# One attention layer with 16 small heads: biases after each half of the scores, row-maximum work at new places, the second half of each load behind the row maxima

## The reference

```python
q, k, v = (layernorm(x) @ W.T + b)                    # 16 heads of 8 columns each
sim  = q k^T + scale * rel_emb[bucket(i - j)]         # causal, 1024 x 1024 for each head
attn = softmax(sim)                                   # row maxima vary: the weights are large
x    = x + (attn @ v) @ Wo.T + bo
h    = relu(layernorm(x) @ w1[0] + b1[0])             # only expert 0 has weight
x    = x + layernorm_gamma_beta(layernorm(x) + h @ w2[0] + b2[0])
```

## Time and profile before

| what | value |
|---|---|
| median of 3 runs | 407.93 us (404.85, 410.7, 407.93) |
| the profiled execution | 402.29 us, of which span 400.5 us |
| PE busy | 321.0 us (80%) |
| DVE busy | 287.5 us (72%) |
| ACT busy | 184.0 us (46%) |
| mean granted TensorE clock | 0.92 of full |

### The profile page before, as it was taken

How to read it: one execution, slowest core, us unless ns; L and a number is a source line. 1 busy time by engine, 2 the same in 40 slices (tenths; PEclk the granted TensorE clock), 3 DMA queues, 4 the chain that set the end, 5 groups by cost and what they waited for, 6 DMA issues and landing times.

```text
span 400.5 us, 8158 instructions
## 1 busy us (share of the span) xinstructions
PE 321.0 (80%) x3197; PEld 153.1 (38%) x3197; DVE 287.5 (72%) x960; ACT 184.0 (46%) x258; POOL 69.5 (17%) x78
## 2 busy tenths in 40 slices
PE   0182438396999899799889979988988998999982
PEld 0131215143334335334434433443443344337752
DVE  3985356358668589588678848967875996773986
ACT  1042024131655554575565545556555545873330
POOL 9812035700001000100100100010010000161552
PEclk9996586668699999999999989999998999999998
DMA  8013422410012101201201220331222010100011
GB/s 227 26 53 116 145 90 95 148 64 3 2 43 66 39 18 52 81 1 61 75 12 44 68 64 2 86 88 26 65 79 55 15 16 12 33 2 10 5 52 53
DMA packets 18295, 21.97 MB, mean 55 GB/s; under 512 B 5584, under 2 KB 14960, under 8 KB 18256
## 3 DMA queue, kind: packets, MB, share of 16 engines
q1 hardware_dynamic: 18256, 21.45, 18.5%
HBM read 14.98 MB, written 4.23 MB: 48 GB/s over the span
## 4 chain that ended last, share of the span: by engine, by line
PE 51%; DVE 17%; DMA 15%; ACT 7%; issue 5%; SPq 4%; POOL 1%; DVEq 0%; POOLq 0%; ACTq 0%
PE ps L1015 14%; PE ps L1044 13%; PE ps L1001 13%; DMA QA<-mrow 7%; ACT PT L626 6%; PE ps L1032 5%; DMA qk_scratch<-QS 4%; DVE FM L759 3%; DVE XN L701 2%; DVE junk L766 2%; DMA KA<-qk_scratch 2%; DMA rows<-in_vectors 2%; PE ps L1077 2%; DVE st L836 1%; DVE U L889 1%
## 5 line engine op out<-in xcount | busy, mean ns | idle before, releaser
L626 ACT ACTIVATE PT<-ps 128x1024 f32<-128x1024 f32 (+1 forms) x192 | 145.8, 810 | 132.4 <-PE ps L1032 101.9
L759 DVE TENSOR_REDUCE FM<-ps 128x1 f32<-128x512 f32 (+3 forms) x176 | 108.4, 660 | 29.2 <-PE ps L1001 29.1
L1001 PE MATMUL ps<-KA,QA 96*128 96x256 bf16 (+3 forms) x544 | 108.7, 294 | 17.6 <-DMA KA<-qk_scratch 14.3
L1015 PE MATMUL ps<-QA,KA 98*128 98x512 bf16 (+3 forms) x384 | 99.0, 343 | 25.4 <-DMA QA<-mrow 10.3
L766 DVE CUSTOM_DVE_ANT_0 junk<-ps,NB 128x256 bf16<-128x256 f32 (+1 forms) x224 | 78.8, 403 | 37.3 <-PE ps L1001 37.2
L1044 PE MATMUL ps<-PT,VG 128*16 128x512 f32 (+3 forms) x768 | 86.9, 498 | 0.0
L1001 PEld LDWEIGHTS ps<-KA,QA 96*128 96x128 bf16 x544 | 44.1, 101 | 103.7 <-DVE FM L759 32.9
L1015 PEld LDWEIGHTS ps<-QA,KA 98*128 98x128 bf16 x384 | 32.5, 101 | 52.5 <-ACT PT L626 21.6
L497 POOL COPY NB<-NBH 128x1024 bf16<-128x1024 bf16 x7 | 7.3, 1040 | 212.3 <-PE ps L1044 211.4
L1032 PE MATMUL ps<-TT,flb 128*32 128x176 f16 (+4 forms) x1152 | 38.9, 245 | 0.0
L1032 PEld LDWEIGHTS ps<-TT,flb 128*32 128x32 bf16 x1152 | 21.5, 96 | 17.9 <-issue 17.0
(11 more groups left out here) (88 smaller groups left out, 255.5 us busy)
## 6 DMA issues: line engine op xcount, KB each, us to landing
QA<-qk_scratch SPq DMA_DIRECT2D x48, 96.0 KB
KA<-qk_scratch SPq DMA_DIRECT2D x16, 288.0 KB
TT<-f_scratch SPq DMA_DIRECT2D x16, 120.0 KB, 7.8
qk_scratch<-QS SPq DMA_DIRECT2D x4, 384.0 KB
qk_scratch<-QS SPq DMA_DIRECT2D x12, 128.0 KB
X<-in_x SPq DMA_DIRECT2D x2, 512.0 KB, 6.2
out<-U SPq DMA_DIRECT2D x4, 256.0 KB, 2.3
xnT<-OT SPq DMA_DIRECT2D x28, 32.0 KB
```

The lines of the kernel that those rows point to most:

```text
L626: nc.scalar.activation(PT[:, s % 3, 2 * q:2 * q + 2, off:off + w], ST[:, q, :, off:off + w], ACT.Exp).then_inc(s_exp, 1)
L759: nc.vector.tensor_reduce(FM[:, ib, heads[0]:heads[-1] + 1, piece], bank[:, 0:w * len(heads)].rearrange("p (h n) -> p h n", n=w), AX.X, AL ...
L1001: last = nc.tensor.matmul(bank[:, i * w + j - j0:i * w + j - j0 + n], QA[0:KS, p, ib // 4, h, (ib % 4) * 128:(ib % 4 + 1) * 128], KA[0:KS, ...
L1015: last = nc.tensor.matmul(ST[:, q, h % 2, off:off + w], KA[0:KST, p, jb // 4, h, (jb % 4) * 128:(jb % 4 + 1) * 128], QA[0:KST, p, ic, h, o ...
```

## The change

1. `biases` takes the half q and is called right after `scores(.., q)`. Before, the biases of both halves came after both score halves.
2. The positions of the units: pos 0 is now after half 0's scores and biases, pos 1 lies behind the values (right ahead of pos 2) and gets nothing from the new planner in the groups 1 to 7, whose cost list is changed with it. With the new constants unit 0 is at (0, 2), unit 10 at (4, 2), units 35 and 36 at (10, 2), unit 37 at (11, 0), and unit 38 alone at the next group's (0, 0). In group 0, whose units are placed by the same even spread as before, unit 37 of group 1 comes to (11, 2).
3. `move_m` is one transfer of two rows.
4. The second half of the load, with TT, of group g + 1 is issued in group g behind the move of group g's half 1. Before, it was issued at the end of group g - 1. Groups 0 and 1 are loaded in full at the start, as before.

```diff
-        half = 2 * step_cols(ic, jb)[1] + (640 if near_cols(ic, jb) else 0)
-        for pos, cost in enumerate((half, half, 4.2 * step_cols(*STEPS[s])[1])):
+        half = 2 * step_cols(ic, jb)[1] + (850 if near_cols(ic, jb) else 0)
+        rest = 4.2 * step_cols(*STEPS[s])[1] + 240
+        for pos, cost in enumerate((half + rest / 2, 0, half + rest / 2)):
...
-S_START, S_END, M1_AT = 0.15, 1.03, 1.06
+S_START, S_END, M1_AT = 0.09, 0.965, 1.0
...
             def move_m(p, half, g):
-                for part in range(2):
-                    sp.dma_start(QA[MROW + part:MROW + part + 1, p, half, :, :],
-                                 mrow[4 * part:4 * part + 4, half, :]).then_inc(s_md[half], 16)
+                sp.dma_start(QA[MROW:MROW + 2, p, half, :, :], mrow[:, half, :]).then_inc(s_md[half], 16)
...
                 move_m(p, 1, g)
+                if g:
+                    second_half(g + 1, (g + 1) % GPB, 1 - p)
                 for k in sums[:1]:
                     gather_all(k)
                 move_m(1 - p, 0, g + 1)
...
-                wait_apart(sp, s_str, 2 * NSTEP * g + 2 * NSTEP)
-                load_half(g + 2, p, 1)
+
+            def second_half(g, hg, p):
+
+                sp.wait_ge(s_str, 2 * NSTEP * (g - 1))
+                load_half(g, p, 1)
                 load_tt(hg, p)
...
             move_m(0, 1, G - 2)
+            second_half(G - 1, GPB - 1, 1)
             gather_all(4)
...
                     if at:
                         scores(*at, 0)
+                        biases(*at[1:], 0)
                     s_units_at(s, 0)
                     if at:
                         scores(*at, 1)
-                    s_units_at(s, 1)
-                    if at:
-                        biases(*at[1:])
+                        biases(*at[1:], 1)
                     if s == 0:
                         pe.wait_ge(s_vg, g + 1)
                     values(g, p, s)
+                    s_units_at(s, 1)
                     s_units_at(s, 2)
```

More of the change, by code:

```diff
@@ L1011, in scores @@
                 if q == 0 and jb == 0:
-                    pe.wait_ge(s_md[ic], 32 * g + 32)
+                    pe.wait_ge(s_md[ic], 16 * g + 16)
                 pe.wait_ge(s_exp, 2 * NSTEP * g + 2 * s + q + 1)
@@ L1020, in scores, with biases @@
                     last.then_inc(s_str, 1)
-            def biases(p, s):
+            def biases(p, s, q):
                 ic, jb = STEPS[s]
@@ L1026, in biases @@
                 near = near_cols(ic, jb)
[L1027 to L1035, removed]
+                if not near:
+                    return
+                for h in range(2 * q, 2 * q + 2):
+                    for c, u0, n in near:
+                        for e in range(2):
+                            r0 = 64 * c + 32 * e
+                            last = nc.tensor.matmul(ST[r0:r0 + 32, q, h % 2, off:off + n], flb[:, 32 * e:32 * e + 32],
+                                                    TT[:, p, h, u0:u0 + n], start=False, stop=True,
+                                                    skip_group_check=True)
+                last.then_inc(s_str, 1)
             def values(g, p, s):
@@ L1155, in _ @@
                 scores(0, 0, 0, q)
+                biases(0, 0, q)
                 unit(0, 0, OWN0 + q)
-            biases(0, 0)
             group(0, 0, 1, first=True)
```

## The result

The changed kernel takes 414.11 us in the median of four runs (413.31 to 415.24); the kernel before, run beside it four times, takes 406.39 us. The ratio is 1.023, with a 95% interval of 1.013 to 1.033. Some executions of a kernel lie over 1.5% above its fastest, and all ratios here leave them out: 1.023 is 414.11 over the 404.85 us of the other three runs of before. The forecast was 405.6 us and no measurable change. The profiled execution took 413.31 us, of which 411.5 us are the span: 11.0 us more than the span of before.

What follows compares the result with a forecast made beforehand. PE was taken as busiest, with holes at seams and row moves. Ahead of the periods - 3.8, six periods + 0.6, behind them + 0.9: - 2.3 us from 407.93 gave 405.6 us; range 394 to 416 us.

Steps and rivals of the forecast that it cites:

- the head: Ahead of the start of group 1's half-1 row move: shorter waits, summing to - 3.8 us.
- the tail: Behind the start of group 7's half-1 row move: more work left, less some waits, + 0.9 us.
- Seam holes and the mrow wait gone: Each period: PE's holes at the seam of two groups (1.25 us) and for the row move (1.6 us) go.
- The load lands at T + 11.5 us, a wait of 2.3 us at unit 10: Groups 1 to 6: load lands 11.5 us after the half-1 row move starts (T); PE needs it at 9.2, waits 2.3.
- I take 0: Splitting biases by half: operand type changes on PE bounded at 0 to 0.1 us a step, taken as 0.
- I add 0.2 us: Ahead of the half-1 row move: PE waits 0.2 us for DVE's maxima, from bounds of 0 and 1 us.
- The period: From one group's half-1 row move start to the next: 32.4 us before the clock is counted, 33.8 us with it.
- The clock, 1.4 us in each of six periods: After the wait at unit 10 the granted clock falls to 0.50, adding 1.4 us to each period.
- Clock kept: Rival: the wait at unit 10 is no longer than 1.42 us, or is borne; 397.2 us, chance 0.17.
- clock stays down: Rival: each wait at unit 10 brings some 9 us at clock 0.50; 424 us, chance 0.15.
- Gathers, 0.8 us in groups 4 to 6: Eight gather transfers right behind the load add 0.8 us to each of these three periods, making 34.6 us.
- The early exponential gives nothing: Rival: at the seam PE waits for the exponential's second half or DVE's maxima instead; 414.0 us, chance 0.08.

Runs made afterwards that it cites:

- POOL's early copy: The changed kernel with POOL's copy of NB released by the end of the group's maxima, ahead of the copy of V: 408.3 us, ratio 1.009.

## Why the prediction was wrong, step by step

The forecast of the periods was + 0.6 us and they took + 9.0; the head was to give 3.8 us and gave 0.1; the tail was to cost 0.9 and cost 2.1. The measured ratio of 1.023 lies above the 2% that the prediction took for the least that can be told, with an interval that begins at 1.013; the time lies inside the range.

- **Seam holes and the mrow wait gone:** right. Both are missing from the timeline in every group from 1 on.
- **The load lands at T + 11.5 us, a wait of 2.3 us at unit 10:** right in mechanism and nearly in size. It lands 11.7 us behind T, and PE is ready about 0.5 us later than at my 9.2; two switches lie in between. The wait is 1.70 to 2.11 us as shown. (The tail of "some 80 GB/s" is that of the windows from 197 to 200, at 76 to 82 GB/s and shares of 0.19 and 0.20; the row quoted for it has 52 GB/s at 0.18.)
- **The split, "I take 0":** this step failed, and it is the largest term. The bounds of 0 to 0.1 us a step were read off a row in which the biases are followed by values. The cost arises when a score matmul or unit follows, and again at the way back into the biases, which the change makes happen nine times a period: 0.15 us each by its busy time, 1.35 us a period, 8.1 us for the six. The upper bound was no bound, because the row did not contain the transition in question.
- **"I add 0.2 us" for DVE at unit 38:** this failed by 0.9 us a period (0.89 us shown, 1.06 with the matmul's overlap), at the upper end of the bounds. The cause was not that the units follow each other more closely but POOL's copy of NB, which the group's last values release, and these now stand behind unit 37. I had followed PE, DVE and SP past the moved units, and not POOL's queue. The bound had been read as a slack of DVE, not as what else runs then.
- **The period:** forecast 32.4 us without the clock, measured 34.85. It shows best in the part behind unit 10, for group 2 of the changed kernel and group 3 of before:

```profile
177.29:200.54 23.25, 22.32 (x250) 8.90 (x254) 19.27 (x56) 12.97 (x16) 1.39 (x2) 1.00 0.08 28
```

```profile
208.49:231.10 22.61, 21.59 (x260) 9.48 (x259) 19.29 (x63) 12.54 (x17) 1.39 (x2) 1.00 0.16 53
```

  Forecast for it were 20.9 us, measured 23.25; T to unit 10 was forecast at 11.5 and took 11.6 us. Of the 2.35 us, 0.86 are unit 38. The remaining 1.5 us are about what the seven switches there cost at 0.2 us each, an attribution by the price above and not measured apart. The two switches ahead of unit 10 cost no time, since PE waits for the load there in any case.
- **The clock, 1.4 us in each of six periods:** the price was right and the count too high. Three periods paid some 1.5 us each (33.68 against 32.20 us busy). This error, 3.9 us, partly hid the two above. "Clock kept" was true in groups 1, 2 and 4 and "clock stays down" in none, though the load move by itself showed it.
- **Gathers, 0.8 us in groups 4 to 6:** too high. Group 4, at full clock, took 35.23 us, 0.4 more than groups 1 and 2; the 1.3 us that the prediction estimated beside it are further off still.
- **Head, - 3.8 us:** failed. The hole of 0.78 us went, and so did the seam holes. But PE waited 2.21 us for DVE ahead of group 0's unit 38, where it had waited 1.75, and 1.44 us ahead of group 1's (POOL's early copy left both as they were, so they have another cause, which is open); and though less work lies ahead of T now, PE was busy 47.6 us from its first scores to T of group 1, 47.2 before. The splits, some of them at half clock, are a likely reason; it was not measured apart.
- **The early exponential gives nothing:** its number, 414.0 us, was met by luck, its mechanism was not. The holes it speaks of did close.

Summed over a period, against before: holes gone, - 1.25 (seam) and - 1.6 us (move); waits new, + 2.0 us (load, with the overlap) and + 1.06 us (DVE); busy, + 1.35 us: + 1.6 us, where 1.5 us was measured (34.85 - 33.35). The clock was down in two periods before and in three after.

Without its load move the change is worth nothing (0.997). With it, it loses 2.3%. Both waits that the change exchanges for each other come from one transfer, whose tail used some 0.19 of the engines' time, three of sixteen. Still open are what the new positions of the units are worth by themselves, and what decides after which wait the clock falls.

## What to carry to other kernels

When a wait behind a transfer is to be moved, first ask why the transfer takes as long as it does: widening one load from three engines was worth 6.0% (of the 23.5 us between the two spans, 10 lie ahead of the periods and 13 in them), while moving its issue only chose who waits for it. A bound for an edit that reorders instructions has to come from a row that contains the new neighbourhood (here, what follows the biases), and a step that is moved has to be checked against every engine that its neighbours' semaphores release, those that are otherwise idle included.

## What was not expected of the hardware

- A lot of bias matmuls (weights of 32 columns, float16 data) that stands between scores or units cost 0.15 to 0.20 us of PE more than one with the values behind it: some 0.1 us going in (0.53 against 0.44 us), and up to 0.16 us coming out (0.32 against 0.16 us for eight). From biases to values nothing shows.
- A cast of 16 elements in a partition took 1.03 us beside POOL's copy of 1.04 us, and 0.17 us alone.
- The length of a wait did not decide whether the granted clock fell: it did after 1.72, 1.87, 2.01 and 2.27 us, and did not after 1.70, 2.11 and 2.73 us. A fall cost 1.4 to 1.5, 2.9 or 4.1 us of PE's busy time.
